# The first of sixteen graphs: adjacency by row block into four free PSUM banks, early weights on ScalarE's queue, inverse roots in two parts

## The chip, the core and the metric

The kernel runs on one core of a Trainium2 chip. A core has TensorE (PE; its weight loads are listed as PEld), VectorE (DVE), ScalarE (ACT), GpSimd (POOL) and SyncE (SP), each with its own instruction stream in program order; they wait for each other by semaphores. Data moves from HBM by DMAs, which are issued from the stream of an engine (SP in the kernel before). The metric is the device time of one execution in microseconds (us); less is better.

## What is computed

Sixteen graphs of 512 nodes and 64 channels pass through four layers, each behind a layer norm and a maximum with 0, each added to x. A batch row is one graph, and the graphs don't depend on each other.

```
h = max(layernorm(x), 0);  x = x + chebyshev(h, adj)   # order 4
h = max(layernorm(x), 0);  x = x + attention(h, adj)   # encoder, 2 attention layers, 3-layer MLP
h = max(layernorm(x), 0);  x = x + gcn(h, adj)
h = max(layernorm(x), 0);  t = adj @ h; x = x + where(t > 0.5, t / t, 0)

chebyshev: d = sum(adj, -1) ** -0.5;  L = I - d[:, None] * adj * d[None, :]
           T0 = I, T1 = L, Tk = 2 L T(k-1) - T(k-2);  out = sum_k Tk @ h @ W[k] + bias
gcn:       rs = sum(adj + I, -1);  di = where(rs > 0, rs ** -0.5, 0)
           out = relu((di[:, None] * (adj + I) * di[None, :]) @ (h @ kernel))
```

## The kernel before, in words

**Tiles.** A graph's adjacency is a_nat, 128 partitions by 4 row blocks by 512 columns (1 MB). TensorE needs it turned: 16 transposes of 128x128 give four column blocks of 128x512, each split into a rounded part at_hi (a copy by ScalarE) and a rest at_lo (a subtraction by VectorE), since products of higher precision are made from both. Slots of three graphs are kept.

**Stages.** A graph passes three rounds. In the first (age 0): norm, turning of adj, row sums and their inverse roots, the products with the Chebyshev weights (cheb_weights), three propagations with folds (cheb_prop3/fold3, prop2/fold2, prop1/fold1), the second norm and the encoder. In the second (age 1): both attention layers. In the third (age 2): MLP, gcn and the last layer. One round handles graph n at age 0, n-1 at age 1 and n-2 at age 2, so in the very first round graph 0 is alone and every engine works on one chain.

**What sets the order.** A table ORDER names, for each engine, the steps of a round in the order in which its stream is written (`turn_a0-0` is turn_a0 of the graph of age 0). `walk` writes them out. Steps of graphs that don't exist in a round are left out.

**Steps named later** (lines of the kernel before). turn_a (L899): four transposes of one column block, from all four row blocks, into bank j % 2 of pre_ps; the third and fourth wait until VectorE has taken the first and second (at_split). copy_at (L521) and row_sum (L535) on ScalarE; row_sum copies a row block and accumulates into rs, and has two records, the ACTIVATE and the read of its accumulator. split_at (L715) on VectorE. Norm: statistics on VectorE (L685 to L691), root and centring on GpSimd (L414, L417), then h_nat and its copy on VectorE (L701, L709). cheb_ht: h is turned (L908), copied (L542) and split (L723). cheb_weights: eight products (L924), then e2, e1, f0 on VectorE (L746 to L749). inverse_roots on GpSimd (L438 to L448): eight small instructions of 128x4, or 128x8 for the power (L441), which makes both d (columns 0 to 3) and di (4 to 7). cheb_u3 on GpSimd (L454 to L462) makes the operand of the first propagation (L936); folds are L953. set_bias_rows (L647 to L658): the value biases of both attention layers, made once, after the first graph's split of its second h_t. Attention: queries L990, keys L995, values L1002 and L1006 with v_n (L580) on ScalarE, scores L1021 to L1025, mask L795 and L803.

**Loads.** SP issues, in this order: x_in and a_nat of graph 0, six early weights (cheb_ws twice, cheb_bs, enc_ws twice, enc_bs; one semaphore early_in), 20 small ones (weights_in), and graphs 1 and 2. Of each weight with 64 rows two copies go to the two partition halves. VectorE's stream begins with a wait for early_in and the splitting of both weights (L668 to L678); only then come the statistics of graph 0.

Of the kernel before, what the change touches and what calls it, by code (L numbers as in the profile page):

```python
# [21 lines left out]
F32 = mybir.dt.float32  # L22
# [36 lines left out]
        norm_cheb-0 add_cheb_bias-0 split_qk.1-1 mask_bias-1 inverse_roots-0 cheb_u3-0  # L59
        norm_gcn-2 split_qk.2-1 cheb_f0-0 norm_last-2 norm_enc-0  # L60
        add_mlp_bias-0""".split(),
# [35 lines left out]
def graph_layers(nc, x, adj, cheb_w, cheb_b, enc_w, enc_b, att_w, att_b, w1, b1, w2, b2, w3, b3,  # L97
# [11 lines left out]
    with ExitStack() as ctx:  # L109
# [112 lines left out]
        weights_split = sem("weights_split")  # L222
        a_loaded = [sem(f"a_loaded{s}") for s in range(SLOTS)]
# [51 lines left out]
        x1b_done = sem("x1b_done")  # L275
        dinv_done = sem("dinv_done")
# [33 lines left out]

        def walk(engine, steps, chains=()):

            order = [(entry[:-2], int(entry[-1])) for entry in ORDER[engine]]
            assert sorted(name for name, _ in order) == sorted(steps), engine

            def one(*graphs):
                for chain in chains:
                    chain.next_round()
                for name, age in order:
# [22 lines left out]
        n_early, n_small = 6, 2 * 6 + 8  # L342
# [4 lines left out]
        def _(sp):  # L347
            early = [(half, cheb_w.rearrange("k o c d -> (o c) k d"))
                     for half in (cheb_ws[0:C], cheb_ws[C:P])]
            early += [(cheb_bs[:], cheb_b.rearrange("a b c -> (a b c)").partition_broadcast(P))]  # L350
            early += [(half, enc_w) for half in (enc_ws[0:C], enc_ws[C:P])]
            early += [(enc_bs[:], enc_b.rearrange("(h o) -> h o", o=1))]
# [10 lines left out]
            assert len(early) == n_early and len(small) == n_small  # L363
# [34 lines left out]
        def _(pool):  # L398
# [32 lines left out]
            def inverse_roots(g):  # L431

                pool.wait_ge(rowsums, 4 * g.n + 4)
                if g.n >= SLOTS:

                    pool.wait_ge(x3_done, g.n - SLOTS + 1)
# [4 lines left out]
                pool_pre.add(gp.tensor_tensor(d[:], rs[:], nhalf[:], ALU.pow))  # L441
# [8 lines left out]
            def cheb_u3(g):  # L450

                pool.wait_ge(dinv_done, g.n + 1)
# [40 lines left out]
            def add_mlp_bias(g):  # L493
# [12 lines left out]
                "inverse_roots": inverse_roots, "cheb_u3": cheb_u3, "cheb_f0": cheb_f0, "norm_enc": scale_norm("pre", 1),  # L506
# [10 lines left out]

# [117 lines left out]
        def _(dve):  # L635
# [38 lines left out]
            for whole, high, low in splits:  # L674
                ve.tensor_copy(high[:], whole).then_inc(weights_split, 1)
# [470 lines left out]
```

## Time and profile before

| | |
|---|---|
| median of three timed runs | 871.86 us (871.08 to 872.88) |
| profiled execution: time, span | 873.75 us, 871.8 us |
| busy: PE, PEld, DVE | 771.5, 543.3, 561.3 us |
| busy: ACT, POOL | 445.4, 357.0 us |
| mean granted TensorE clock | 0.969 of 2.4 GHz |

The span runs from the first to the last instruction record; the execution's own time is 1.95 us longer, and the profiled execution lies 1.89 us above the median. In the steady part one round takes 49.0 us. Rounds 2 to 16 each take in a new graph; two rounds behind them drain.

A row of the timeline reads: start in us, duration, engine and line, operation, output tile <- input tiles, shapes, count, and in brackets the idle time of that engine just before it and what ended it. SPq marks the issue of a DMA. Durations of matmuls include their latency; where they follow each other the starts tell the pace.

### The profile page before, as it was taken

The page shows a single profiled execution, that of the slowest core. Times are in us where ns is not written, and L with a number is a line of the kernel's source. Part 1 is how long each engine was busy: PE and PEld are TensorE (multiplying, and loading weights), DVE is VectorE, ACT ScalarE, POOL GpSimd, SP SyncE. Part 2 cuts the span into 40 slices and gives each one's busy share as a digit, 9 for nine tenths or more (in the row PEclk, how much of TensorE's full clock was granted, in tenths as well). Part 3 has the DMA queues.
Part 4 walks back from the last instruction along what each step waited for, and adds up shares of the span by engine and source line. Part 5 has one row for each costly group of instructions (what it writes and reads, how often), then busy time and mean ns, then how long its engine had stood idle before and what let it go on. Part 6 is the DMA issues. An engine that isn't in the chain of part 4 may idle for free.

```text
span 871.8 us, 11510 instructions
## 1 busy us (share of the span) xinstructions
PE 771.5 (88%) x3808; PEld 543.3 (62%) x3808; DVE 561.3 (64%) x1631; ACT 445.4 (51%) x929; POOL 357.0 (41%) x475
## 2 busy tenths in 40 slices
PE   3649799998999999998999999998999999998864
PEld 2426566675766766675766666675766666675533
DVE  3255667767676767767676767767676767765432
ACT  2035463737474563737474563737474563735430
POOL 3133434536162544536162544536162544532200
PEclk9869899999999999999999999999999999999995
DMA  6100100102010010201020010101020110000000
GB/s 166 45 0 1 43 14 1 61 1 61 1 61 2 21 41 0 61 1 61 1 62 1 18 44 1 61 1 62 1 61 1 18 44 1 7 1 6 1 7 6
DMA packets 29275, 22.77 MB, mean 26 GB/s; under 512 B 19488, under 2 KB 21024, under 8 KB 29216
## 3 DMA queue, kind: packets, MB, share of 16 engines
q1 hardware_dynamic: 29216, 22.03, 8.5%
q8 instruction: 31, 0.51, 0.2%
q14 instruction: 28, 0.23, 0.1%
HBM read 19.93 MB, written 2.10 MB: 25 GB/s over the span
## 4 chain that ended last, share of the span: by engine, by line
PE 52%; issue 16%; POOL 15%; DVE 12%; ACT 4%; POOLq 0%; DVEq 0%
PE turn_ps L1056 13%; PE pre_ps L936 8%; PE post_ps L936 4%; POOL rstd_pre L414 4%; PE pre_ps L953 4%; PE turn_ps L1039 3%; POOL k_lo L486 2%; PE pre_ps L899 2%; DVE h_nat_pre L709 2%; POOL centred_pre L417 2%; DVE score_ps L795 2%; PE qkv_ps L990 2%; DVE h_nat_pre L701 2%; PE qkv_ps L995 2%; PE post_ps L1071 2%
## 5 line engine op out<-in xcount | busy, mean ns | idle before, releaser
L589 ACT ACTIVATE negz<-negz,negmax 128x512 f32<-128x512 f32 x128 | 92.2, 720 | 63.9 <-DVE negmax L803 63.8
L414 POOL TENSOR_TENSOR rstd_post<-vareps_post,nhalf 128x4 f32<-128x4 f32 x32 | 32.8, 1024 | 209.6 <-DVE vareps_post L691 209.6
L1056 PE MATMUL turn_ps<-pt,v_n 128*128 128x512 f32 x256 | 115.2, 592 | 0.0
L795 DVE TENSOR_TENSOR score_ps<-score_ps,a_nat 128x512 f32<-128x512 f32 x128 | 89.1, 696 | 19.4 <-PE score_ps L1025 18.5
L936 PE MATMUL pre_ps<-at_hi,u_pair_pre 128*128 128x512 f32 x192 | 88.4, 461 | 7.2 <-DVE u_pair_pre L731 5.2
L548 ACT ACTIVATE y_t_pre<-pre_ps 128x512 f32<-128x512 f32 x48 | 28.7, 597 | 124.6 <-PE pre_ps L936 124.6
L803 DVE CUSTOM_DVE_ANT_0 negz<-score_ps,gate 128x512 f32<-128x512 f32 x128 | 88.6, 692 | 4.4
L414 POOL TENSOR_TENSOR rstd_pre<-vareps_pre,nhalf 128x4 f32<-128x4 f32 x32 | 33.9, 1060 | 130.7 <-DVE vareps_pre L691 130.7
L596 ACT ACTIVATE pt<-turn_ps 128x512 f32<-128x512 f32 x128 | 74.0, 592 | 17.7 <-PE turn_ps L1039 15.6
L1039 PEld LDWEIGHTS turn_ps<-ident,negz 128*128 128x128 f32 x512 | 61.1, 141 | 32.6 <-issue 16.1
L936 PE MATMUL pre_ps<-at_lo,u_pair_pre 128*128 128x512 f32 x192 | 79.3, 413 | 0.0
L1039 PE MATMUL turn_ps<-ident,negz 128*128 128x128 f32 x512 | 75.9, 276 | 1.9 <-ACT negz L589 1.7
L1056 PEld LDWEIGHTS turn_ps<-pt,v_n 128*128 128x128 f32 x256 | 46.1, 190 | 45.9 <-issue 45.9
L936 PE MATMUL post_ps<-at_hi,u_pair_post 128*128 128x512 f32 x128 | 55.7, 435 | 21.5 <-DVE u_pair_post L731 21.5
L486 POOL TENSOR_TENSOR q_lo<-q_t,q_hi 128x512 fp32r<-128x512 f32 x32 | 43.6, 1363 | 67.1 <-ACT q_t L566 67.1
L1021 PE MATMUL score_ps<-k_hi,q_hi 128*128 128x512 f32 x128 | 63.6, 497 | 6.2 <-DVE negmax L803 6.2
L486 POOL TENSOR_TENSOR k_lo<-k_t,k_hi 128x512 fp32r<-128x512 f32 x32 | 45.9, 1435 | 45.9 <-ACT k_t L566 45.9
L899 PE MATMUL pre_ps<-ident,a_nat 128*128 128x128 f32 x256 | 41.2, 290 | 20.6 <-DVE at_lo L715 13.3
L899 PEld LDWEIGHTS pre_ps<-ident,a_nat 128*128 128x128 f32 x256 | 31.4, 148 | 42.3 <-issue 42.3
L715 DVE TENSOR_TENSOR at_lo<-pre_ps,at_hi 128x512 fp32r<-128x512 f32 x64 | 42.7, 685 | 21.6 <-ACT at_hi L521 21.5
L814 DVE TENSOR_TENSOR h_t<-turn_ps,inv_row 128x512 f32<-128x512 f32 x32 | 22.1, 692 | 50.7 <-PE turn_ps L1056 50.7
L1024 PE MATMUL score_ps<-k_lo,q_hi 128*128 128x512 f32 x128 | 52.6, 411 | 1.6 <-POOL k_lo L486 1.6
(138 smaller groups left out, 1791.5 us busy)
## 6 DMA issues: line engine op xcount, KB each, us to landing
a_nat<-in_adj SPq DMA_DIRECT2D x16, 1024.0 KB, 5.8
x_in<-in_x SPq DMA_DIRECT2D x16, 128.0 KB, 2.6
out<-x_out SPq DMA_DIRECT2D x16, 128.0 KB, 1.9
cheb_ws<-in_L_gnn_weight SPq DMA_DIRECT2D x2, 64.0 KB, 4.9
att_w<-in_L_gnn_a_wv SPq DMA_DIRECT2D x2, 64.0 KB, 2.5
att_w<-in_L_gnn_a_wk SPq DMA_DIRECT2D x2, 64.0 KB, 2.3
att_w<-in_L_gnn_a_wq SPq DMA_DIRECT2D x2, 64.0 KB, 2.2
bv_f<-in_L_gnn_a_bv SPq DMA_DIRECT2D x2, 64.0 KB, 2.7
```

The costliest lines, as they stand in the source:

```text
L414: gp.tensor_tensor(rstd[t][:], vareps[t][:], nhalf[:, 0:RB], ALU.pow)\
L486: gp.tensor_tensor(low[a][:], whole[:], high[a][:].bitcast(F32), ALU.subtract)\
L589: sc.activation(probs[:, i, :], negz[:, i, :], ACT.Exp, bias=negmax[:, i:i + 1], scale=-1.0, accum_out=total[:, i:i + 1]).then_inc(probs_d ...
L596: sc.activation(pt[:, :, i * P:(i + 1) * P], turn_ps[i % 2][:].rearrange("p (j n) -> p j n", n=P), ACT.Copy)\
L795: ve.tensor_tensor(score_ps[i % 2][:], score_ps[i % 2][:], a_nat[s][:, i, :], ALU.mult)\
L803: ve.tensor_tensor_reduce(negz[:, i, :], score_ps[i % 2][:], gate[:, i, :], -1.0, 3.0e38, ALU.add, ALU.min, negmax[:, i:i + 1]).then_inc(b ...
L899: mm = te.transpose(pre_ps[:, j % 2, i * P:(i + 1) * P], a_nat[g.slot][:, i, j * P:(j + 1) * P], ident[:])
L936: mm = te.matmul(bank, u_pair[t][:, j, :, :].rearrange("p a c -> p (a c)"), at[g.slot][:, j, :], start=(j == 0 and at is at_hi), stop=(j = ...
L1021: te.matmul(score_ps[i % 2][:], q_hi[a][:, part], k_hi[a][:], start=True, stop=False)
L1024: te.matmul(score_ps[i % 2][:], q_hi[a][:, part], k_lo[a][:], start=False, stop=False)
L1039: mm = te.transpose(turn_ps[i % 2][:, j * P:(j + 1) * P], probs[:, i, j * P:(j + 1) * P], ident[:])
L1056: mm = te.matmul(turn_ps[0][:], v_n[a][:, j * P:(j + 1) * P], pt[:, j, :], start=(j == 0), stop=(j == RB - 1))
```

## The change

For graph 0 alone there is a second table, FIRST, with the same steps in another order, used in the first round. In it:

- adj comes in four DMAs, one a row block, each with its own semaphore. TensorE turns a row block when it has landed, into four banks (post_ps, qkv_ps, turn_ps0, turn_ps1), which nothing else uses in this round. The first h is turned into score_ps0. So no turn waits for a split, and all at_lo come due at cheb_prop3.
- ScalarE sums three row blocks, copies h_t, sums the fourth, and then makes the four at_hi.
- The six early weights are issued from ScalarE's stream, ahead of its table load, with a semaphore of their own for cheb_ws.
- VectorE begins with the norm; the Chebyshev weights are split behind it, the encoder's behind fold3, and the value biases of layer 1 behind fold3, of layer 2 behind fold2.

For all graphs, inverse_roots is split: `roots` makes d (a power of 128x4), cheb_u3 follows at once, and `more_roots` makes di and the rest behind it (a second power of 128x4). cheb_weights on VectorE waits for root_done, fold3 for dinv_done.

```diff
+FIRST = {
+    "tensor": """
+        turn_a0-0 turn_a1-0 turn_a2-0 cheb_ht-0 turn_a3-0 cheb_weights-0 cheb_prop3-0 cheb_fold3-0
...
-        norm_cheb-0 add_cheb_bias-0 split_qk.1-1 mask_bias-1 inverse_roots-0 cheb_u3-0
+        norm_cheb-0 add_cheb_bias-0 split_qk.1-1 mask_bias-1 roots-0 cheb_u3-0 more_roots-0
...
+        def at_bank(g, j):
+            return (post_ps, qkv_ps, *turn_ps)[j][:] if first(g) else pre_ps[:, j % 2, :]
+        def ht_bank(g, k):
+            return score_ps[0][:] if first(g) and k == 0 else pre_ps[:, 0, :]
...
-            load(Graph(0, 0), False)
+            sp.dma_start(x_in[0][:], x_d[0]).then_inc(x_loaded[0], 16)
+            for i in range(RB):
+                sp.dma_start(a_nat[0][:, i, :], adj_d[0][:, i, :]).then_inc(a_rows_in[i], 16)
...
-            for to, what in early:
-                sp.dma_start(to, what).then_inc(early_in, 16)
...
+            def roots(g):
+                pool.wait_ge(rowsums, 4 * g.n + 4)
+                gp.tensor_tensor(dinv[g.slot][:, 0:RB], rs[:, 0:RB], nhalf[:, 0:RB], ALU.pow)\
+                    .then_inc(root_done, 1)
...
-                pool_pre.add(gp.tensor_tensor(d[:], rs[:], nhalf[:], ALU.pow))
+                pool_pre.add(gp.tensor_tensor(d[:, RB:], rs[:, RB:], nhalf[:, RB:], ALU.pow))
...
+            for half in (cheb_ws[0:C], cheb_ws[C:P]):
+                act.dma_start(half, cheb_w.rearrange("k o c d -> (o c) k d")).then_inc(cheb_in, 16)
+            for to, what in early:
+                act.dma_start(to, what).then_inc(early_in, 16)
...
+            def turn_first_rows(g, i):
+                wait_rows(pe, g, i)
+                for j in range(RB):
+                    mm = te.transpose(at_bank(g, j)[:, i * P:(i + 1) * P],
+                                      a_nat[g.slot][:, i, j * P:(j + 1) * P], ident[:])
+                    if i == RB - 1:
+                        mm.then_inc(at_ready, 1)
...
             def cheb_prop3(g):
+                if first(g):
+                    pe.wait_ge(at_split, RB)
```

Three places in the streams show it. First VectorE's stream in graph 0, before: from the split of the weights to e2 (at_lo0 is the rest of graph 0's turned adj, h_t the turned h).

```order
L678 TENSOR_TENSOR cheb_lo<-cheb_ws,cheb_hi 128x192 [waits weights_split]
L678 TENSOR_TENSOR enc_lo<-enc_ws,enc_hi 128x128
L685 BN_STATS stats_pre<-x_in0 128x6 [waits x_loaded0]
L685 BN_STATS stats_pre<-x_in0 128x6 x3
L688 BN_AGGR meanvar_pre<-stats_pre 128x2 [waits dve_pre]
L688 BN_AGGR meanvar_pre<-stats_pre 128x2 x3
L691 TENSOR_SCALAR vareps_pre<-meanvar_pre 128x4 [waits dve_pre]
L701 SCALAR_TENSOR_TENSOR h_nat_pre<-centred_pre,rstd_pre 128x4x64 [waits rstd_done_pre]
L709 COPY h_nat_pre<-h_nat_pre 128x4x64 [waits dve_pre]
L715 TENSOR_TENSOR at_lo0<-pre_ps,at_hi0 128x512 [waits at_copied] x4
L723 TENSOR_TENSOR h_t<-pre_ps,h_t 64x512 [waits ht_copied]
L746 TENSOR_TENSOR e2<-pre_ps,dinv0 128x256 [waits dinv_done,cheb_ready]
```

The same stretch of VectorE's stream now; the norm stands ahead of these rows.

```order
L720 SCALAR_TENSOR_TENSOR cheb_ws<-cheb_ws 128x64 [waits cheb_in]
L722 TENSOR_TENSOR cheb_ws<-cheb_ws 128x64
L712 CAST cheb_hi<-cheb_ws 128x192 [waits weights_split]
L714 TENSOR_TENSOR cheb_lo<-cheb_ws,cheb_hi 128x192 [waits weights_split]
L772 TENSOR_TENSOR h_t<-score_ps0,h_t 64x512 [waits ht_copied]
L764 TENSOR_TENSOR at_lo0<-post_ps,at_hi0 128x512 [waits at_copied]
L764 TENSOR_TENSOR at_lo0<-qkv_ps,at_hi0 128x512 [waits at_copied]
L795 TENSOR_TENSOR e2<-pre_ps,dinv0 128x256 [waits root_done,cheb_ready]
L796 TENSOR_TENSOR e1<-pre_ps,dinv0 128x256
L798 TENSOR_TENSOR f0<-pre_ps,x_b 128x256 [waits xb_done]
L764 TENSOR_TENSOR at_lo0<-turn_ps0,at_hi0 128x512 [waits at_copied]
L764 TENSOR_TENSOR at_lo0<-turn_ps1,at_hi0 128x512 [waits at_copied]
```

The weights moved from ahead of the norm to behind it, h_t moved ahead of all at_lo, and two at_lo stand behind f0.

Second, ScalarE's stream in graph 0, before: the last at_hi and row sum (junk, rs), then h_t and the copies of the propagations.

```order
L521 ACTIVATE at_hi0<-pre_ps 128x512 [waits at_ready]
L535 ACTIVATE junk,rs<-a_nat0 128x512 [waits rowsums]
L542 ACTIVATE h_t<-pre_ps 128x512 [waits ht_ready]
L548 ACTIVATE y_t_pre<-pre_ps 128x512 [waits y_ready_pre] x3
L542 ACTIVATE h_t<-pre_ps 128x512 [waits ht_ready]
```

ScalarE's stream from its last early DMA to the first propagations' copies now:

```order
L563 DMA enc_bs<-in_L1_gnn_enc_b 128x1
L583 ACT_TABLE_LOAD
L583 ACTIVATE junk,rs<-a_nat0 128x512 [waits a_rows_in0]
L583 ACTIVATE junk,rs<-a_nat0 128x512 [waits rowsums,a_rows_in1]
L583 ACTIVATE junk,rs<-a_nat0 128x512 [waits rowsums,a_rows_in2]
L590 ACTIVATE h_t<-score_ps0 128x512 [waits ht_ready]
L583 ACTIVATE junk,rs<-a_nat0 128x512 [waits rowsums,a_rows_in3]
L568 ACTIVATE at_hi0<-post_ps 128x512 [waits at_ready]
L568 ACTIVATE at_hi0<-qkv_ps 128x512 [waits at_ready]
L568 ACTIVATE at_hi0<-turn_ps0 128x512 [waits at_ready]
L568 ACTIVATE at_hi0<-turn_ps1 128x512 [waits at_ready]
L596 ACTIVATE y_t_pre<-pre_ps 128x512 [waits y_ready_pre] x3
```

All four at_hi now stand behind h_t and the four row sums.

Third, GpSimd's stream in graph 0 before, from x_b (x plus bias) to the operand u_pair_pre; the rows from L438 on come again for every graph.

```order
L428 TENSOR_TENSOR x_b<-x_in0,cheb_bs 128x256 [waits early_in,x_loaded0]
L438 TENSOR_SCALAR rs<-rs 128x4 [waits rowsums]
L439 TENSOR_SCALAR positive<-rs 128x4
L441 TENSOR_TENSOR dinv0<-rs,nhalf 128x8 [waits pool_pre]
L443 TENSOR_TENSOR dinv0<-dinv0,positive 128x4 [waits pool_pre]
L444 TENSOR_SCALAR d_neg<-dinv0 128x4
L445 TENSOR_TENSOR d_root<-dinv0,rs 128x4
L446 TENSOR_SCALAR d_m2<-dinv0 128x4
L448 TENSOR_TENSOR d_m2<-d_m2,dinv0 128x4 [waits pool_pre]
L454 TENSOR_TENSOR u3<-h_nat_pre,dinv0 128x256 [waits h_ready_pre,dinv_done]
L460 CAST u_pair_pre<-u3 128x4x64 [waits pool_pre]
L462 TENSOR_TENSOR u_pair_pre<-u3,u_pair_pre 128x4x64 [waits pool_pre]
```

GpSimd's stream there now (one more row, the last d_m2, follows):

```order
L460 TENSOR_TENSOR x_b<-x_in0,cheb_bs 128x256 [waits early_in,x_loaded0]
L466 TENSOR_TENSOR dinv0<-rs,nhalf 128x4 [waits rowsums]
L491 TENSOR_TENSOR u3<-h_nat_pre,dinv0 128x256 [waits h_ready_pre,root_done]
L497 CAST u_pair_pre<-u3 128x4x64 [waits pool_pre]
L499 TENSOR_TENSOR u_pair_pre<-u3,u_pair_pre 128x4x64 [waits pool_pre]
L475 TENSOR_SCALAR rs<-rs 128x4
L476 TENSOR_SCALAR positive<-rs 128x4
L478 TENSOR_TENSOR dinv0<-rs,nhalf 128x4 [waits pool_pre]
L480 TENSOR_TENSOR dinv0<-dinv0,positive 128x4 [waits pool_pre]
L481 TENSOR_SCALAR d_neg<-dinv0 128x4
L482 TENSOR_TENSOR d_root<-dinv0,rs 128x4
L483 TENSOR_SCALAR d_m2<-dinv0 128x4
```

The three instructions of u3 moved from behind all the roots to behind the first power.

## Rows read from the trace of the kernel before

**Rows 1.** The page's head: span of the profiled execution.
```profile
span 871.8 us, 11510 instructions
```
**Rows 2.** Chain that ended last: start us, us, what.
```profile
23.86 3.77 PE pre_ps L936 x8
...
124.68 1.86 PE pre_ps L936 x8
```
**Rows 3.** Stretch 40 to 60 us: busy of engines, PEclk granted, DMA share, GB/s.
```profile
40.00:60.00 20.00, 11.18 (x30) 6.83 (x30) 9.40 (x42) 3.63 (x6) 3.06 (x5) 0.52 0.00 0
```
**Rows 4.** Timeline of all engines, 0 to 23 us.
```profile
0.72 1.28 ACT L521 ACT_TABLE_LOAD   x1 [0.72 <-PEq L1130]
0.72 0.45 SPq L370 DMA_DIRECT2D x_in<-in_x  x1
...
7.27 1.94 PE L899 MATMUL pre_ps<-ident,a_nat 128*128 128x128 f32 x8 [7.27 <-DMA a_nat<-in_adj]
...
8.55 0.23 DVE L668 SCALAR_TENSOR_TENSOR cheb_ws<-cheb_ws 128x64 f32<-128x64 f32 x1 [5.33 <-DMA enc_bs<-in_L_gnn_enc_b]
...
9.86 0.60 DVE L685 BATCH_NORM_STATS2 stats_pre<-x_in 128x6 f32<-128x64 f32 x4
...
11.15 1.03 POOL L414 TENSOR_TENSOR rstd_pre<-vareps_pre,nhalf 128x4 f32<-128x4 f32 x1 [8.19 <-DVE vareps_pre L691]
...
13.77 0.29 DVE L709 COPY h_nat_pre<-h_nat_pre 128x256 f32<-128x256 f32 x1
...
14.81 1.94 PE L899 MATMUL pre_ps<-ident,a_nat 128*128 128x128 f32 x8 [5.60 <-DVE at_lo L715]
...
17.31 1.11 PE L908 MATMUL pre_ps<-ident,h_nat_pre 128*128 128x128 f32 x4 [0.56 <-DVE at_lo L715]
17.52 0.63 ACT L535 ACTIVATE junk<-a_nat 128x512 bf16<-128x512 f32 x1
...
18.46 0.60 ACT L542 ACTIVATE h_t<-pre_ps 128x512 fp32r<-128x512 f32 x1 [0.23 <-PE pre_ps L908]
...
18.98 1.66 POOL L441 TENSOR_TENSOR dinv<-rs,nhalf 128x8 f32<-128x8 f32 x1
...
19.84 0.53 PE L924 MATMUL pre_ps<-cheb_hi,h_t 128*128 128x192 f32 x1 [1.42 <-DVE h_t L723]
...
21.91 0.42 DVE L746 TENSOR_TENSOR e<-pre_ps,dinv 128x256 f32<-128x256 f32 x1 [2.12 <-PE pre_ps L924]
```
**Rows 5.** DMA view, issues from 0 to 1 us: KB each, us from issue to landing.
```profile
x_in<-in_x SPq DMA_DIRECT2D x1, 128.0 KB, 2.3
```
**Rows 6.** Waits, 0 to 60 us: in total, times, longest us.
```profile
DVE tmp L777 <- PE pre_ps L953: 6.5, 1, 6.5
...
DVE tmp L766 <- PE pre_ps L953: 5.2, 1, 5.2
```
**Rows 7.** Timeline of the second round, 53 to 68 us.
```profile
53.78 0.71 DVE L647 CAST bv_rows<-bv_f 1x128 bf16<-1x128 f32 x3
...
59.43 0.59 DVE L685 BATCH_NORM_STATS2 stats_pre<-x_in 128x6 f32<-128x64 f32 x4
...
63.33 1.24 DVE L709 COPY h_nat_pre<-h_nat_pre 128x256 f32<-128x256 f32 x1
...
63.44 0.60 ACT L580 ACTIVATE v_n<-qkv_ps 128x512 f32<-128x512 f32 x1
...
65.44 1.66 PE L899 MATMUL pre_ps<-ident,a_nat 128*128 128x128 f32 x8 [2.18 <-DVE at_lo L715]
...
67.83 0.69 DVE L715 TENSOR_TENSOR at_lo<-pre_ps,at_hi 128x512 fp32r<-128x512 f32 x1 [0.40 <-ACT at_hi L521]
```
**Rows 8.** Timeline of a steady round, 314 to 321 us.
```profile
314.97 0.69 DVE L803 CUSTOM_DVE_ANT_0 negz<-score_ps,gate 128x512 f32<-128x512 f32 x1
...
315.70 0.73 POOL L462 TENSOR_TENSOR u_pair_pre<-u,u_pair_pre 128x256 fp32r<-128x256 f32 x1
...
320.56 0.48 PE L936 MATMUL pre_ps<-at_hi,u_pair_pre 128*128 128x512 f32 x1
```

More of the change, by code:

```diff
@@ L318, in one @@
                     chain.next_round()
-                for name, age in order:
+                for name, age in fill if graphs[1:] == (None, None) else order:
                     g = graphs[age]
@@ L347, in _ @@
         def _(sp):
[L348 to L352, printed above, removed]
             small = []
@@ L362, in _ @@
             small += [(half, gcn_w) for half in (gcn_ws[0:C], gcn_ws[C:P])]
-            assert len(early) == n_early and len(small) == n_small
+            assert len(small) == n_small
             def load(g, waits=True):
@@ L516, in _ @@
             sc = nc.scalar
+            early = [(cheb_bs[:], cheb_b.rearrange("a b c -> (a b c)").partition_broadcast(P))]
+            early += [(half, enc_w) for half in (enc_ws[0:C], enc_ws[C:P])]
+            early += [(enc_bs[:], enc_b.rearrange("(h o) -> h o", o=1))]
+            assert len(early) == n_early
+            for half in (cheb_ws[0:C], cheb_ws[C:P]):
+                act.dma_start(half, cheb_w.rearrange("k o c d -> (o c) k d")).then_inc(cheb_in, 16)
+            for to, what in early:
+                act.dma_start(to, what).then_inc(early_in, 16)
             def copy_at(j):
@@ L526, in f @@
                 def f(g):
+                    if i == 0 or first(g):
+                        wait_rows(act, g, i)
                     if i == 0:
-                        act.wait_ge(a_loaded[g.slot], 16 * (g.round + 1))
                         if follows(g):
@@ new lines, in set_bias_rows, with split_weights @@
+                for i in range(1, RB):
+                    ve.tensor_copy(bv_rows[a][0:96, i, :], bv_rows[a][0:96, 0, :])\
+                        .then_inc(bias_rows, 1)
+                    made += 1
+                assert made == (a + 1) * n_bias_rows // 2
+            def split_weights(whole, high, low, made):
+                ve.tensor_copy(high[:], whole).then_inc(weights_split, 1)
+                dve.wait_ge(weights_split, made + 1)
+                ve.tensor_tensor(low[:], whole, high[:].bitcast(F32), ALU.subtract)\
+                    .then_inc(weights_split, 1)
@@ L673, in _ @@
-            splits = ((cheb_ws[:, 0:K - 1, :], cheb_hi, cheb_lo), (enc_ws[:], enc_hi, enc_lo))
-            for whole, high, low in splits:
-                ve.tensor_copy(high[:], whole).then_inc(weights_split, 1)
-            dve.wait_ge(weights_split, 5)
-            for whole, high, low in splits:
-                ve.tensor_tensor(low[:], whole, high[:].bitcast(F32), ALU.subtract)\
-                    .then_inc(weights_split, 1)
             def norm_stats(t, chain, g, k, src):
@@ L722, in split_ht @@
                 dve.wait_ge(ht_copied, 2 * g.n + k + 1)
-                ve.tensor_tensor(h_t[C:P, :], pre_ps[C:P, 0, :], h_t[C:P, :].bitcast(F32),
+                ve.tensor_tensor(h_t[C:P, :], ht_bank(g, k)[C:P, :], h_t[C:P, :].bitcast(F32),
                                  ALU.subtract).then_inc(ht_split, 1)
-                if first(g) and k == 1:
-                    set_bias_rows()
             def split_u(t, chain, u):
@@ L739, in cheb_norm @@
                 norm_apply("pre", dve_pre, g, 0)
+                if first(g):
+                    combine_cheb_weights()
             def cheb_weights(g):
@@ L770, in cheb_fold2 @@
                 split_u("pre", dve_pre, c1)
+                if first(g):
+                    set_bias_rows(1)
             def cheb_fold1(g):
```

123 lines of the change are left out of this document (77 added, 46 removed).

## Prediction

> **What bounds the kernel now.** I read the page's head first, then the chain that ended last, since only time on that chain can be won. The span is 871.8 us [rows 1]; the table ahead gives PE as busy for 771.5 of it, and the chain runs through TensorE in the steady rounds. The change hardly touches these rounds, so the second view is the timeline of the start, where graph 0 is alone. There nothing is full: one chain hops over the engines until the first propagation (L936) starts at 23.86 [rows 2]. The rows to see, in order [rows 4]: x_in is issued at 0.72 and lands 2.3 later [rows 5], so at 3.0, but VectorE stands still 5.33 us until 8.55 for enc_bs, the last of the early weights, and takes up x_in only at 9.86. Adj has landed at 7.27, TensorE turns two column blocks, and then waits 5.60 us, until 14.81, for at_lo, which stands behind the norm in VectorE's stream (the norm's last piece starts at 13.77). Behind that come h_t, the Chebyshev products and e2 at 21.91. The third view is the second round [rows 7]: VectorE makes the bias rows from 53.78, so the norm of graph 1 begins at 59.43, its last copy ends at 64.57, and TensorE waits 2.18 us until 65.44 for the at_lo behind it.
>
> From 40 to 60 us the granted clock is 0.52, that is nearly all at the 1.2 GHz level [rows 3]. The first propagation takes 3.77, a later one 1.86 [rows 2]: by that pace it ran at the same level. I keep the start at it throughout.
>
> **Term 1: the start of the first propagation.** All durations are those of [rows 4] unless another group is named.
>
> VectorE: statistics can start at 3.3, when x_in is there and the cast of ident is done. From their start to the end of the norm's copy before: 9.86 to 14.06, so 4.2. The h is ready at 7.5. Four of the six weight instructions follow; all six took 9.86 - 8.55 = 1.3, so I give them 1.0, to 8.5. They are needed only for the products, two microseconds later.
>
> Transfers: adj landed at 7.27, the early weights at 8.55. The 1.28 between them is what the early weights cost behind adj. Now they compete with it. If none of them gets ahead of the last row block it lands at 7.2, if all do at 8.5; I take 7.9, and 7.0 for the third. In these rows the transfers of one queue only are seen, so the share is my choice of the middle.
>
> For that place the Trainium skill, page "DMA: Bandwidth & Descriptors", section "Issuing engines are not separate DMA queues", says that DMAs from different engines run on the same 16 DMA engines and interleave, and that issuing from several saves only the time of issuing. The trace before has one queue and can't show it; the rule speaks against the move of the early weights, and by it the last block would stand at the late end, 8.5, and the sum below would lose nothing to 0.5.
>
> TensorE: a row block takes 0.97 (half of 1.94). The third is turned at 8.0. h is turned from 8.0, with ScalarE's copy 1.15 after the start of the turn (18.46 - 17.31): copy from 9.15 to 9.75. The fourth block is turned meanwhile, to about 10.
>
> ScalarE: six issues of DMAs stand ahead of its table load. Nearest row is SP's issue of x_in, 0.45; up to 0.7 each as bound. So 0.7 + 2.7 to 4.2, and 1.28 for the table: free at 4.7 to 6.2. A row sum is 0.63 and its accumulator 0.2, three are 2.5: done at 8.7 at the latest, before the copy of h_t at 9.15. The fourth ends at 10.5. Four at_hi of 0.6, which overlap by 0.1, end at 12.6.
>
> VectorE: split of h_t 9.75 to 10.45 (0.69 as at_lo [rows 7]). TensorE's eight products took 19.84 to 21.91, so 2.1: to 12.55. In this time two at_lo are made. Then e2, e1, f0, three of 0.42 with overlap and wait, 1.1: to 13.65. Then two at_lo, 1.3: to 14.95. The first propagation starts at 15.0.
>
> GpSimd: power of 128x4 from 10.5, 1.03 by the row of rstd (L414); the three of u3 before ended at about 23.8 and began after d_m2, 2.0: ready at 13.6. VectorE is later, so GpSimd hides behind it with 1.4 to spare.
>
> 23.86 - 15.0 = 8.9. Bounds: 7.5, if every choice above is at its late end, and 9.7, if transfers cost nothing and VectorE finds all at_hi waiting.
>
> **Term 2: bias rows out of the second round.** They take 59.43 - 53.78 = 5.65. Their halves, 2.8 each, and the encoder's split (0.5) go into VectorE's waits of 5.2 (before L766) and 6.5 (before L777) [rows 6]. 3.3 in 5.2 and 2.8 in 6.5 fit: nothing, as long as the clock is low. In the second round the norm is then done at 53.8 + 4.2 = 58.0 instead of 64.57. What is late next is ScalarE: its stream has v_n from 63.44 to 64.04 ahead of the third at_hi, and TensorE has its values ahead of the third turn. Before, the third turn began at 65.44 and its copy some 0.65 later, at 66.1; now the copy can begin at 63.95. So the last at_lo (67.83) comes 2.1 earlier, and with it the first mask. I take 2.0 of the 5.65; bounds 1.0 and 2.7. These times are all on the old clock of the start; they come 8.9 earlier.
>
> **Term 3: roots in two parts, 16 graphs.** One power of 1.66 becomes two of 1.03, +0.4 on GpSimd a graph. In a steady round the operand is ready at 316.43 and TensorE takes it at 320.56 [rows 8]: 4.1 us to spare, before and after. So 0. Bounds: 0 to +0.4 a graph, 6 in all, if GpSimd's stream set the round; I take the cover of 4.1 and go by 0. DMAs of graphs 1 and 2 start some 2.7 earlier, as six issues have left SP's queue, and are needed 30 us later: 0.
>
> The moved three instructions of u3 now lie beside other work of VectorE. The row that warns is the copy at 63.33, which takes 1.24 beside GpSimd's work instead of 0.29 [rows 4, 7]. Where they lay before, L803 kept its 0.69 beside them [rows 8], and 2.2 us earlier come a multiplication by inv_row and the same L795 and L803, all with an operand in PSUM: 0. In graph 0, x_b can fall onto the weight split: at most 0.7, and between its end at 8.5 and the products at 10.45 there is 1.9 to spare.
>
> The Trainium skill, "SBUF — State Buffer", section "SBUF: two separate sides", has the rule: GpSimd and a VectorE instruction with two SBUF inputs or in a two-port mode lock each other out of a shared port for the whole instruction. By that rule, too, the three instructions cost nothing beside VectorE's reads of PSUM; the 1.24 of the copy agrees with it.
>
> **Sum.** 8.9 + 2.0 + 0 = 10.9. Against the profiled execution: span 871.8 - 10.9 = 860.9, and with the 1.95 around it 862.85. That execution is 1.89 above the median of the runs, so the median is forecast at 871.86 - 10.9 = 861.0 us.
>
> **Rivals.**
> (A) The transfers hold the start. With pieces of adj and early weights mixed, the third row block lands at 9 instead of 7. Then h_t is turned at 10 and all behind it is 2 later. For it: adj needed 7.27 even alone at the head of its queue. Against it: the third block needs only three quarters of adj to be through. Gain 8 to 9: 863.4.
> (B) The clock. The start before ran at the low level. A denser TensorE could get the high level earlier. A propagation is then 3.77 - 1.86 = 1.9 shorter; two of them on the chain give 3.8, less some 0.5 since the bias rows no longer fit into VectorE's wait. 857.7. For it: the turns, h_t and products are packed into 8 us. Against it: the chain of three propagations, with its gaps, is the same, and the level was low with it from 40 to 60.
> (C) Slower: the three instructions of u3, moved by 2.2 us in each steady round, lock out VectorE on the path from attention's multiplication to the mask. Price by the copy's rows: 1.24 - 0.29 = 0.95 a graph, in 15 graphs 14.3, less the 10.9: 875.3. It decides from 0.73 a graph. Against it speaks L803's 0.69 beside the same three instructions.
> (D) The change doesn't do what it says: the first propagation starts as before, since another wait ends last (early weights from ScalarE land as late as 8.5 and the Chebyshev split with them, with the table load and row sums behind). But even with all of them at 8.5 the start is 16.5, so little is left for it: 871.
>
> **How the numbers follow.** Forecast 0.62, A 0.17, B 0.13, C 0.04, D 0.04. The forecast's own spread comes from 7.5 to 9.7 and 1.0 to 2.7, so 859.5 to 863.4. For 8 in 10 I go on half way into B at the low side and over A at the high side: 858.5 to 864.3. What a measurement of this kernel can tell from no change is about 0.2%, 1.7 us. Faster: forecast, A, B, 0.92; the same: D, 0.04; slower: C, 0.04.
>
> **What would show it.** In the profile after: statistics of graph 0 at about 3.3; h turned at about 8; the first propagation at 15.0, released by VectorE's last at_lo and not by GpSimd or a DMA; no bias rows behind the second h_t; the norm of graph 1 finished before its first at_hi; last at_lo of graph 1 some 11 us earlier than 67.83; steady rounds of 49.0 us as before. It is wrong if a row block's DMA releases the h_t turn late (A), if a propagation before 40 us takes under 3 us (B), if the round is longer than 49.1 (C), or if the first propagation starts after 17 (D).

## The result, and the profile after

The changed kernel takes 860.58 us (median of 4 runs, 858.40 to 862.05) against 872.02 for the kernel before on the same chip: a ratio of 0.987 (95% interval 0.984 to 0.989), 11.4 us faster. The forecast was 861.0, from 10.9. The profiled execution after has a span of 859.1. One execution of the kernel with the roots in one part (below), 1093.49 us at a granted clock of 0.652, is a slow run and is left out of that kernel's median.

The start is read first. The timeline of the kernel after, graph 0, all engines (start, duration, engine, line; in brackets the idle time before and what ended it):

```profile
3.32 0.61 DVE L734 BATCH_NORM_STATS2 stats_pre<-x_in 128x6 f32<-128x64 f32 x4
4.65 1.28 ACT L583 ACT_TABLE_LOAD   x1 [4.65 <-issue]
5.09 0.45 PE L950 MATMUL post_ps<-ident,a_nat 128*128 128x128 f32 x1 [5.09 <-DMA a_nat<-in_adj]
...
6.74 0.29 DVE L758 COPY h_nat_pre<-h_nat_pre 128x256 f32<-128x256 f32 x1
...
8.03 0.47 PE L950 MATMUL post_ps<-ident,a_nat 128*128 128x128 f32 x1 [1.00 <-DMA a_nat<-in_adj]
...
8.94 1.06 PE L976 MATMUL score_ps<-ident,h_nat_pre 128*128 128x128 f32 x4
...
10.04 0.60 ACT L590 ACTIVATE h_t<-score_ps 128x512 fp32r<-128x512 f32 x1 [1.30 <-PE score_ps L976]
10.67 0.69 DVE L772 TENSOR_TENSOR h_t<-score_ps,h_t 64x512 fp32r<-64x512 f32 x1 [2.68 <-ACT h_t L590]
11.32 1.02 POOL L466 TENSOR_TENSOR dinv<-rs,nhalf 128x4 f32<-128x4 f32 x1 [1.42 <-ACT junk L583]
11.42 0.53 PE L994 MATMUL pre_ps<-cheb_hi,h_t 128*128 128x192 f32 x1 [0.56 <-DVE h_t L772]
...
13.48 0.42 DVE L795 TENSOR_TENSOR e<-pre_ps,dinv 128x256 f32<-128x256 f32 x1 [0.42 <-PE pre_ps L994]
13.59 0.73 POOL L499 TENSOR_TENSOR u_pair_pre<-u,u_pair_pre 128x256 fp32r<-128x256 f32 x1
...
14.48 1.28 DVE L764 TENSOR_TENSOR at_lo<-turn_ps,at_hi 128x512 fp32r<-128x512 f32 x2
15.81 0.79 PE L1006 MATMUL pre_ps<-at_hi,u_pair_pre 128*128 128x512 f32 x1 [2.38 <-DVE at_lo L764]
```

Against [rows 4]: VectorE takes up x_in at 3.32 instead of 9.86, and h is ready at 7.03. TensorE turns two row blocks from 5.09 and stands still 1.00 for the third, so the gap of 5.60 for at_lo is gone. The first propagation starts at 15.81 instead of 23.86, released by VectorE's last at_lo, with GpSimd's operand ready 1.5 earlier (14.32).

TensorE behind it, in the same execution: the first fold and the queries, the first products of graph 0's attention.

```profile
20.28 1.97 PE L1023 MATMUL pre_ps<-cheb_ws,y_t_pre 128*128 128x64 f32 x8 [0.69 <-ACT y_t_pre L596]
...
48.10 2.04 PE L1064 MATMUL qkv_ps<-h_t,att_w 128*128 128x512 f32 x2 [0.93 <-ACT h_t L606]
```

The queries of the kernel before:

```profile
55.96 2.04 PE L990 MATMUL qkv_ps<-h_t,att_w 128*128 128x512 f32 x2 [0.93 <-ACT h_t L558]
```

VectorE in the second round of the kernel after:

```profile
24.67 0.70 DVE L694 CAST bv_rows<-bv_f 1x128 bf16<-1x128 f32 x3
...
31.62 1.68 DVE L694 CAST bv_rows<-bv_f 1x128 bf16<-1x128 f32 x3
...
45.92 0.60 DVE L734 BATCH_NORM_STATS2 stats_pre<-x_in 128x6 f32<-128x64 f32 x4
...
49.83 0.29 DVE L758 COPY h_nat_pre<-h_nat_pre 128x256 f32<-128x256 f32 x1
52.02 0.69 DVE L764 TENSOR_TENSOR at_lo<-pre_ps,at_hi 128x512 fp32r<-128x512 f32 x1 [1.90 <-ACT at_hi L568]
...
57.80 0.69 DVE L764 TENSOR_TENSOR at_lo<-pre_ps,at_hi 128x512 fp32r<-128x512 f32 x1 [0.41 <-ACT at_hi L568]
58.41 0.69 DVE L851 TENSOR_TENSOR score_ps<-score_ps,a_nat 128x512 f32<-128x512 f32 x1
```

The bias rows now lie at 24.67 and 31.62, in VectorE's waits. The last at_lo stands at 57.80; in [rows 7] it stands at 67.83. Of the 10.03 between them 7.86 were won before (queries at 48.10, before 55.96), so the second round gives 2.17 in this pair. The first mask (L851) starts at 58.41. The copy at 49.83 takes 0.29; in [rows 7] it took 1.24, beside GpSimd's work.

The rest: from graph 0's x_out (its output) to graph 13's are 637.00 us, or 49.00 a round (before 637.43, or 49.03). The profiled pair is 12.7 apart (871.8 and 859.1), more than the medians. Of that, 10.0 lie ahead of the first mask, 1.5 between it and graph 0's x_out (84.25 and 85.75), 0.4 in the 13 rounds, and 0.8 behind them, where the last fold took 1.10 after and 1.97 before. The 1.5 isn't put down to the change: the same stretch takes 83.92 in one kernel with the old order below and 85.0 in two with the new one.

### The profile page after: what moved, and what is told of

The parts are those of the page before. It is cut to its first block, busy times and chain, and to the rows that moved or that the text cites. A ratio compares the mean times of both kernels' runs of the same rounds, so it can differ in the third digit from the quotient of the medians.

```text
span 859.1 us, 11501 instructions
## 1 busy us (share of the span) xinstructions
PE 764.4 (89%) x3776; PEld 540.5 (63%) x3808; DVE 560.9 (65%) x1631; ACT 445.9 (52%) x929; POOL 364.0 (42%) x491
## 4 chain that ended last, share of the span: by engine, by line
PE 53%; issue 15%; POOL 14%; DVE 12%; ACT 5%; DMA 1%; POOLq 0%; SPq 0%; ACTq 0%; DVEq 0%
PE turn_ps L1130 13%; PE pre_ps L1006 8%; PE post_ps L1006 4%; PE pre_ps L1023 4%; POOL rstd_pre L446 3%; PE turn_ps L1113 3%; POOL k_lo L523 2%; PE qkv_ps L1064 2%; PE pre_ps L967 2%; DVE h_nat_pre L758 2%; POOL centred_pre L449 2%; DVE score_ps L851 2%; PE qkv_ps L1069 2%; PE post_ps L1145 2%; PE pre_ps L994 2%
## 5 line engine op out<-in xcount | busy, mean ns | idle before, releaser
L851 DVE TENSOR_TENSOR score_ps<-score_ps,a_nat 128x512 f32<-128x512 f32 x128 | 89.1, 696 | 18.9 <-PE score_ps L1099 18.0
L764 DVE TENSOR_TENSOR at_lo<-pre_ps,at_hi 128x512 fp32r<-128x512 f32 x60 | 40.1, 685 | 22.9 <-ACT at_hi L568 22.9
L1006 PE MATMUL post_ps<-at_lo,u_pair_post 128*128 128x512 f32 x128 | 52.3, 408 | 0.0
L1099 PE MATMUL score_ps<-k_hi,q_lo 128*128 128x512 f32 x128 | 50.7, 396 | 0.0
```

What stands on the lines that cost most here:

```text
L851: ve.tensor_tensor(score_ps[i % 2][:], score_ps[i % 2][:], a_nat[s][:, i, :], ALU.mult)\
L1006: mm = te.matmul(bank, u_pair[t][:, j, :, :].rearrange("p a c -> p (a c)"), at[g.slot][:, j, :], start=(j == 0 and at is at_hi), stop=(j = ...
L1099: te.matmul(score_ps[i % 2][:], q_lo[a][:, part], k_hi[a][:], start=False, stop=True)\
```

## The experiments

Each starts from the changed kernel unless said otherwise. Times are medians.

**One part put back: early weights behind the row blocks, all from SyncE**

```
-                act.dma_start(half, cheb_w...)   # and four more, on ScalarE
+                sp.dma_start(half, cheb_w...)    # behind the four a_rows
```

> The changed kernel, but the six early weights are issued by SyncE right behind the four row blocks of the adjacency instead of by ScalarE beside them. Theory (the early weights share the transfers and held the third row block until 8.03 us): the third block is turned at 7.0 or before, ScalarE's table load starts at about 0.7 instead of 4.65, and the first propagation starts at 14.8 instead of 15.81, so the time is some 0.9 us under the changed kernel, 859.7. Rival 1 (the adjacency is as late without them): third block still at 8.0, start 15.8, same time. Rival 2 (the weights now land too late for VectorE's split, which the Chebyshev products need by 11.4): products after 11.8, start later than 15.8, time 861 to 862.

Measured: 859.12 us. Its timeline, TensorE:

```profile
6.76 0.48 PE L949 MATMUL post_ps<-ident,a_nat 128*128 128x128 f32 x1
...
8.27 0.27 PE L949 MATMUL post_ps<-ident,a_nat 128*128 128x128 f32 x1
...
13.72 0.50 PE L1005 MATMUL pre_ps<-at_hi,u_pair_pre 128*128 128x512 f32 x1 [2.74 <-DVE at_lo L763]
...
15.13 0.63 PE L1005 MATMUL pre_ps<-at_lo,u_pair_pre 128*128 128x512 f32 x1
```

The third row block is turned at 6.76 instead of 8.03: issued beside the adjacency, the early weights had cost it 1.3 us in this pair. The landing itself varies: in the six kernels here with the weights on ScalarE's queue an engine takes up the third block at 7.57 to 8.12, in the three with the weights behind the rows at 6.74, 6.14 and 6.04. The two groups don't overlap, so the cost is shown, and its size is 0.8 to 2.1. The propagation starts 2.09 earlier, of which 1.27 is the block; the rest comes with a pace nobody had forecast: a turn of 128 columns takes 0.27 from 8.27 on instead of 0.42, and the first four matmuls of the propagation are fast, the others slow. (The next kernel has its products at this pace too, and its propagation starts at 14.83, so against it 1.1 are left.) By time the two kernels can't be told apart (1.5 us; ratios to before 0.985 and 0.987, with intervals that overlap), so the theory is shown by the landing and not by the median. Rival 2 is excluded: VectorE did wait for the Chebyshev weights until 7.89, and the products still began at 9.85.

**One part put back: bias rows behind the second h_t**

```
-                    set_bias_rows(0)        # in cheb_fold3; (1) in cheb_fold2
+                if first(g) and k == 1:     # in split_ht, as before
+                    set_bias_rows(0)
+                    set_bias_rows(1)
```

> The changed kernel, but both halves of the bias rows are made behind the second split of h_t of graph 0 again, where they stood before. Theory: the first propagation stays at 15.8, queries at 48.1 or a little earlier; the norm of graph 1 then waits for them and the first mask comes at 60.6 instead of 58.4: 2.2 us slower than the changed kernel, 862.8. Rival 1 (they cost nothing in the second round, the clock's later start made the difference): first mask 58.4, same time. Rival 2 (the piece that ran slowly beside GpSimd in VectorE's waits held the encoder's norm): queries over 0.5 earlier than 48.1 and a cost of 1.7 or less.

Measured: 861.85 us, 1.3 over the changed kernel. Its VectorE:

```profile
43.77 0.71 DVE L694 CAST bv_rows<-bv_f 1x128 bf16<-1x128 f32 x3
...
49.42 0.59 DVE L734 BATCH_NORM_STATS2 stats_pre<-x_in 128x6 f32<-128x64 f32 x4
...
53.32 1.24 DVE L758 COPY h_nat_pre<-h_nat_pre 128x256 f32<-128x256 f32 x1
...
58.83 0.69 DVE L851 TENSOR_TENSOR score_ps<-score_ps,a_nat 128x512 f32<-128x512 f32 x1
```

The norm of graph 1 starts behind them and the 1.24 of the copy is back. From queries to first mask are 12.88 instead of 10.31, 2.6 more. But this execution reached its queries 2.15 earlier (45.95). The kernel with two waits in the other order (below) has the rows where the changed kernel has them, its queries as early (45.72), and 11.73 to the mask; against it the late rows cost 1.15. The mechanism is shown; its size is 1.1 to 2.6, with 1.3 in the median. The time falls under rival 2, but its reason doesn't hold, since the earlier queries aren't VectorE freed of the rows: 0.98 of the 2.15 lie ahead of the first propagation (14.83), 0.30 are its last matmuls and 0.87 one more fold at the fast pace (1.10 instead of 1.97 for eight products).

**Banks without the row blocks: turned by column, once all has landed**

```
-    wait_rows(pe, g, i); for j: ...at_bank(g, j)[:, i*P:...]
+    if i == 0: wait for all four; for i: ...at_bank(g, j)[:, i*P:...]
```

> The changed kernel, but graph 0's adjacency is turned by column block into the four free banks once all four row blocks are there, instead of by row block as they land. Transfers, banks and VectorE's order are as in the changed kernel. Theory: the last block lands at about 8.8, three columns take 2.6, so h_t is turned at 11.4 instead of 8.94, and all behind it comes 2.5 later: first propagation 18.3, time 863.1. Rival (VectorE's order and ScalarE's copies set the start, the turns have slack): first propagation within 0.5 of 15.8, time within 0.5 of the changed kernel.

Measured: 863.71 us, TensorE released so:

```profile
8.57 1.09 PE L952 MATMUL post_ps<-ident,a_nat 128*128 128x128 f32 x4 [8.57 <-DMA a_nat<-in_adj]
...
18.03 0.80 PE L1007 MATMUL pre_ps<-at_hi,u_pair_pre 128*128 128x512 f32 x1 [2.37 <-DVE at_lo L764]
```

2.2 later at the propagation and 3.1 in the median: turning as the blocks land is worth 2 to 3 us here. (The intervals of the two ratios, 0.987 to 0.993 and 0.984 to 0.989, overlap at their ends, so the propagation is the better evidence.) The turns have no slack.

**The order of VectorE alone, in the kernel before**

```
-            dve.wait_ge(early_in, 16 * n_early)   # and the six weight instructions, ahead of all graphs
+                if first(g): weights_ready()       # the same, behind graph 0's norm
```

> The kernel before, with one edit: VectorE combines and splits the early weights behind the norm of graph 0 instead of ahead of its statistics. Two banks, whole adjacency in one transfer, weights by SyncE. Theory (order on VectorE gives about half of the 8.05 us): statistics at 3.3, weights split from 8.55 to 9.9, first at_lo to 10.6, third turn at 10.6 instead of 14.81, first propagation 4.2 earlier, 19.7, time 867.8. Rival 1 (the wait for at_lo was only nominal, the banks and the transfer set the start): less than 2 us. Rival 2 (order is nearly all of it): first propagation before 17.5, 6 us or more.

Measured: 868.65 us, 3.5 under the kernel before. Its VectorE and TensorE:

```profile
3.15 0.60 DVE L686 BATCH_NORM_STATS2 stats_pre<-x_in 128x6 f32<-128x64 f32 x4
...
8.83 0.23 DVE L669 SCALAR_TENSOR_TENSOR cheb_ws<-cheb_ws 128x64 f32<-128x64 f32 x1 [1.97 <-DMA enc_bs<-in_L_gnn_enc_b]
...
11.53 1.94 PE L902 MATMUL pre_ps<-ident,a_nat 128*128 128x128 f32 x8 [1.71 <-DVE at_lo L716]
...
20.59 0.77 PE L939 MATMUL pre_ps<-at_hi,u_pair_pre 128*128 128x512 f32 x1 [2.01 <-POOL u_pair_pre L462]
```

The wait for at_lo shrinks from 5.60 to 1.71, the propagation comes 3.27 earlier. It fell 0.9 short of the expectation: the adjacency landed at 7.88, the weights at 8.83, and one weight instruction took 0.78 instead of about 0.2. So of the 8.05 of the start, VectorE's order alone makes 3.3 and turning row by row 2.2; the remaining 2.6 belong to the free banks, the earlier root and the transfers. These two runs don't tell them apart; the next one prices the root at 1.0 to 2.0, and the early weights' queue takes something off again. What the free banks alone are worth isn't shown. Nor need the parts add up: one edit was put into the kernel before, the others taken out of the changed one.

**Roots in one part again**

```
-    dinv[:, 0:RB] = pow(rs) ; then_inc(root_done)      # roots
-    ... d[:, RB:] = pow(rs[:, RB:])                     # more_roots
+    ... d[:] = pow(rs[:]) ...                           # one chain, waits on dinv_done
```

> The changed kernel with the inverse roots of all 16 graphs taken in one part again (one power of 8 columns, and u3, e2 and e1 wait for the whole chain of GpSimd's small operations). Theory: in graph 0 the operand of the first propagation is ready 2.0 later than 14.32, at 16.3, so the first propagation starts 0.5 later; the steady round goes from 49.00 back to 49.03, which is 0.45 us in 13 rounds; together 1.0 us slower than the changed kernel. Rival 1 (the split has nothing to do with the shorter round): round stays 49.00, 0.5 us slower. Rival 2 (the second power costs on GpSimd): round 48.97 or less, not slower.

Measured: 860.92 us (859.75 to 861.81, 4 runs), 0.3 over the changed kernel. Its VectorE and TensorE:

```profile
14.47 0.43 DVE L789 TENSOR_TENSOR e<-pre_ps,dinv 128x256 f32<-128x256 f32 x1 [1.81 <-POOL d_m L479]
...
16.81 0.79 PE L999 MATMUL pre_ps<-at_hi,u_pair_pre 128*128 128x512 f32 x1 [4.65 <-DVE at_lo L758]
```

The operand is ready at 16.32, as expected, but it isn't what ends last: e has to wait for the whole chain, until 14.47, and the two at_lo behind it end at 16.76. The propagation starts 1.0 later than in the changed kernel. Against the kernel with late bias rows, which had its third row block as early (7.57, here 7.64) and its products at the same pace, it is 2.0 later (14.83). So the split is worth 1.0 to 2.0 at the start, not 0.5. The steady round is 48.98, not 49.03: the shorter round isn't the roots'. In the medians, 0.3 apart with an interval of about 2 us, nothing of this can be seen, and the expected 1.0 is neither confirmed nor excluded.

**Two waits in the other order**

```
-                    if j >= 2: pe.wait_ge(at_split, ...)
                     wait_rows(pe, g, 0)
+                    if j >= 2: pe.wait_ge(at_split, ...)
```

> The changed kernel with one edit that touches no computation: from graph 1 on, TensorE's third and fourth turn of the adjacency wait for the adjacency first and for at_lo second, as in the kernel before (in the changed kernel it is the other way round). Theory (this order makes the 0.05 us by which the steady round is shorter, since TensorE waits there for at_lo): round 49.03 to 49.04 instead of 48.98 to 49.00, and 0.6 us slower. Rival (the round is shorter for another reason): round 49.00 or less.

Measured: 860.93 us, round 49.03. TensorE's third turn in a steady round, of this kernel and then of the changed one:

```profile
295.13 1.23 PE L967 MATMUL pre_ps<-ident,a_nat 128*128 128x128 f32 x8 [0.41 <-DVE at_lo L764]
```

```profile
295.80 1.26 PE L967 MATMUL pre_ps<-ident,a_nat 128*128 128x128 f32 x8 [0.32 <-DVE at_lo L764]
```

The wait is 0.09 longer when at_lo stands second in the code, and the round 0.034 longer (637.44 over 13 rounds against 637.00). The other profiles agree: the median of this wait over the steady rounds is 0.40 or 0.41, and the round 49.03 to 49.04, in the four kernels that wait for the adjacency first; it is 0.31 or 0.32, and the round 48.98 to 49.00, in the eight that wait for at_lo first. So this side effect of rewriting turn_a makes the 0.4 us; the medians, 0.35 apart, can't resolve it.

**TensorE's waits filled**

```
+            def fill(g, n):          # graph 0 only: 4 to 60 ahead of a wait, 202 in all
+                for _ in range(n):
+                    te.matmul(score_ps[1][:, 0:P], ones_bf[:], ones_bf[:], ...)
```

> The changed kernel with TensorE's waits in graph 0's first passage filled by products of ones_bf with itself (128 columns, some 190 in all) into a bank that nobody reads then; results are unchanged. Theory (TensorE runs at the 1.2 GHz pace in the first 50 us because it stands still between short stretches of work, as rival B had it): the three propagations take 1.9 instead of 3.8, folds and the encoder's products halve too, queries start 8 to 9 us before 48.1, and the time is 7 to 10 us under the changed kernel, 852. Rival 1 (the level does not follow from the work in these waits): paces as in the changed kernel, and the fillers that overrun a wait make it 1 to 4 us slower. Rival 2 (the gain is given back later by a longer stretch at 1.2 GHz): queries much earlier, but the distance between first mask and the end longer, gain under 3.

Measured: 852.89 us, 7.7 under the changed kernel. Its TensorE:

```profile
14.52 0.50 PE L1013 MATMUL pre_ps<-at_hi,u_pair_pre 128*128 128x512 f32 x1 [1.73 <-DVE at_lo L764]
14.85 0.39 PE L1013 MATMUL pre_ps<-at_lo,u_pair_pre 128*128 128x512 f32 x1
15.09 0.40 PE L1013 MATMUL pre_ps<-at_hi,u_pair_pre 128*128 128x512 f32 x1
...
20.21 0.50 PE L1013 MATMUL pre_ps<-at_hi,u_pair_pre 128*128 128x512 f32 x1 [0.65 <-DVE u_pair_pre L778]
```

The windows of TensorE (busy time of each engine, then the granted clock), of the changed kernel and then of the filled one:

```profile
5.00:30.00 25.00, 17.41 (x60) 13.48 (x60) 11.04 (x34) 7.45 (x16) 7.22 (x15) 1.00 0.52 152
...
32.00:50.00 18.00, 9.74 (x25) 6.04 (x26) 9.31 (x37) 1.88 (x3) 5.49 (x8) 0.50 0.00 0
```

```profile
32.00:50.00 18.00, 12.28 (x109) 9.08 (x106) 8.77 (x27) 9.18 (x20) 10.26 (x11) 1.00 0.00 0
```

The propagations run at the 2.4 GHz pace (matmuls of 512 columns 0.23 to 0.24 apart instead of 0.43, and 2.1 for a propagation instead of 3.8) and the queries come at 39.29 instead of 48.10. The theory holds: 8.8 at the queries, 9.8 at the first mask, 7.7 in the median, where no run of this kernel (851.08 to 853.36) is as long as the shortest of the changed one (858.40). Where the 2 us between mask and median went isn't shown. So the low pace of this start followed from TensorE standing still in its waits; the next run shows that filling them doesn't always prevent it.

**Both: early weights behind the row blocks, and fillers**

The two edits above together.

> The same fillers on the kernel whose early weights are issued by SyncE behind the row blocks. There the products of graph 0 and half of its first propagation already ran at the 2.4 GHz pace (0.24 us for 512 columns, 0.43 behind 15.1). Theory: the level stays high from about 8 us on, queries 8 us before that kernel's 44.0, and 7 to 9 us under its 859.1: 851. Rival 1: no change of pace, 859 to 862. Rival 2 (given back later): queries early, gain under 3.

Measured: 850.10 us (849.65 to 854.10, 5 runs), 9.0 under the one without fillers and the best median of all: ratio to the kernel before 0.976 (0.974 to 0.978). The level isn't sure: in the profiled execution, the slowest of the five (854.10), the first propagation ran at the slow pace (matmuls 0.43 apart from 14.01 on), and the queries, at 40.33, are later than with fillers alone. The kernel of the next experiment has the same first round, and its profile has the fast pace throughout, with queries at 38.56:

```profile
13.77 0.50 PE L1012 MATMUL pre_ps<-at_hi,u_pair_pre 128*128 128x512 f32 x1 [1.72 <-DVE at_lo L763]
...
38.56 1.10 PE L1082 MATMUL qkv_ps<-h_t,att_w 128*128 128x512 f32 x2 [0.47 <-ACT h_t L605]
```

**Fillers in the last graph too**

This one starts from the kernel just above, with 148 more fillers in the last graph.

```
+                fill(g, 8, B - 1)    # ahead of each MLP product; 56 ahead of a propagation, 6 ahead of a fold
```

> The kernel with early weights behind the row blocks and fillers in graph 0, and in addition fillers in TensorE's waits of the last graph, from its MLP to its last fold (148 products of 128 columns in the same bank, free by then). Theory (the pace of 0.43 us for 512 columns behind 827 us comes from those waits, as at the start): the last two propagations take 1.9 instead of 3.8, the last part, from graph 14's output to graph 15's, goes from 34.6 to 31, and the time is 3 us under 850.1: 847. Rival 1 (fillers overrun the waits and give that back): 849 to 851. Rival 2 (the level at the end has another cause, such as the high load of the 700 us before): pace unchanged, no gain.

Measured: 850.97 us (849.38 to 851.11). Its last propagation and fold:

```profile
838.78 0.50 PE L1012 MATMUL post_ps<-at_hi,u_pair_post 128*128 128x512 f32 x1 [2.03 <-DVE u_pair_post L777]
...
840.78 0.63 PE L1012 MATMUL post_ps<-at_lo,u_pair_post 128*128 128x512 f32 x1
...
842.10 1.97 PE L1029 MATMUL post_ps<-fold,y_t_post 128*128 128x64 f32 x8
```

From graph 14's x_out to graph 15's are 32.73 instead of 34.57 (34.3 to 35.4 in all the kernels without these fillers), so 1.8 of the 3 expected, until the level falls at 840.3 in spite of the fillers. In the median nothing is seen: 0.9 over the 850.10, inside the band of rival 1, whose cause no row shows. Inconclusive as to time.

**The kernel before, filled**

The same edit on the kernel before, with 34 fillers ahead of the first turn, 42 ahead of the third and 15 ahead of the first propagation, 249 in all.

> The kernel before with fillers in TensorE's waits of graph 0 (some 215, more in the two long waits there), results unchanged. It holds the clock equal on both sides of the comparison with the changed kernel with fillers (852.89). Theory (the change's gain is its start and its second round, and the clock adds or takes little on average): before with fillers 863 to 864, 10 to 11 over the filled changed kernel, first propagation at 22 to 23 with a pace of 0.24. Rival 1 (a good part of the 11.4 us was a better clock with the change): below 861. Rival 2 (fillers gain less in before, so the change and the fillers work together): above 866.

Measured: 866.59 us (863.67 to 867.14, 6 runs), 5.6 under the kernel before. Its TensorE:

```profile
14.62 1.68 PE L905 MATMUL pre_ps<-ident,a_nat 128*128 128x128 f32 x8 [3.61 <-DVE at_lo L715]
...
24.27 0.63 PE L943 MATMUL pre_ps<-at_hi,u_pair_pre 128*128 128x512 f32 x1
...
25.44 0.40 PE L943 MATMUL pre_ps<-at_lo,u_pair_pre 128*128 128x512 f32 x1
```

Rival 2 came true, narrowly (its bound was 866). The long wait was left with 3.61 us unfilled (the 42 fillers ran through it fast, in 2.51), the granted clock was 0.50 from 15 to 25, and the first propagation starts at 23.28, half of it at the slow pace. Filled, the two kernels are 13.7 apart, unfilled 11.4. So a better clock with the change doesn't explain its gain (rival 1): 8.8 of the 13.7 lie at the first propagation, 1.3 between it and the queries, where only this kernel has slow matmuls, and from queries to first mask are 9.36 us in the filled changed kernel and 12.45 here, 3.1 where the change's second term gave 2.2 at the slow pace. Fillers sized for this kernel's waits weren't tried.

## Why the prediction was right, step by step

**The bound.** Right: the chain over the engines in the start was where the time could be won.

**Term 1 was mis-sized, 8.05 instead of 8.9.** The failing step is the share of the early weights in the transfers, which I had said was "my choice of the middle": the third block came at 8.03 and not at 7.0. Behind it the forecast distances held: h_t turned at 8.94 (8.0), its copy at 10.04 (9.15), products done at 13.44 (12.55), last at_lo done at 15.76 (14.95). The offset stays at 0.8 to 0.9 all the way. So the truth lay between the forecast and rival A, which had the block at 9. The weights on ScalarE's queue are a part of the change that costs time: with them behind the rows in one queue the block was turned 1.27 earlier.

The rule of the Trainium skill, "DMA: Bandwidth & Descriptors", section "Issuing engines are not separate DMA queues", that DMAs from different engines interleave on the same 16 DMA engines, was the better guide: by it I had put the last block at 8.5, and in the kernel turned by column, with the same transfers, TensorE had all four at 8.57.

One distance was too long and hidden: the norm took 3.7 and not 4.2, since h_nat's first instruction took 0.43 instead of 0.93, so h was ready at 7.03 and waited for the third block. ScalarE was free at 5.93, inside 4.7 to 6.2, and hidden as forecast. GpSimd was ready at 14.32 instead of 13.6, 1.5 before VectorE; with the roots in one part the start is 1.0 to 2.0 later, by e and not by the operand.

**Term 2: 2.17 instead of 2.0**, by the landmarks of the two profiles. The halves fitted into the waits; 2.05 and 2.30 of wait were left behind them. Three casts together took 1.68 beside a subtraction and a product by GpSimd (0.70 otherwise) and were hidden too. What was late next was ScalarE's at_hi, as said. But the 2.17 hold for one pace only. In the kernel before and in the two made from it (VectorE's order alone, and filled), queries to first mask take 12.45 to 12.49, whatever TensorE's pace. With the new order it is TensorE's pace that sets it: 11.73 and 11.76 where queries and keys both ran slow, 10.3 to 10.6 where the queries did and the keys mostly not, 9.4 with both fast. So the term is worth 0.7 to 3.1, and that the two profiles to be compared had the same pace there was luck.

**Term 3: 0 for the roots was right** for the steady rounds. Rival C is excluded, since the round didn't grow (49.00). Not foreseen were the 0.4 us of the two waits in turn_a.

**Rival B** had the wrong cause for this kernel and the right lever. In its profile the denser start didn't lift the pace (0.43 from 16.4 to 27; one fold of three fast, as before). In near copies it did in part: the one with two waits swapped had all three folds fast, and the one with the early weights behind the rows had a first propagation of 2.89, under B's sign of 3. The whole level could be had, for 7.7 us, by filling waits.

**The sum**: 8.05 + 2.17 + 0.43 = 10.65, against 11.4 measured by medians with an interval of about 2 us either way. That the total came within 0.5 of the forecast is in part luck: term 1 was 0.85 too large, and 0.17 of term 2 and the 0.43 of the two waits, which nobody had in the sum, made up for most of it.

## What to carry to other kernels

When a start-up chain hops over engines, take the distances behind the first landing from the rows, and spend the care on the landing: they held to 0.2 us while the landing was off by 1.0. Small transfers that are needed later belong behind the large one that is needed first, not on another engine's queue: here that brought the landing 0.8 us or more forward, which the medians could not resolve. And where TensorE waits in short gaps at a program's start, look at the spacing of equal matmuls: here idle waits at the start cost 7.7 us, nearly as much as the whole change had won there. Before a difference between two profiles is put down to an edit, compare the pace of equal matmuls in both.

## What the runs showed of the hardware

In the first 30 us of the changed kernel the granted clock reads 1.00, while matmuls of 512 columns come 0.43 apart, the pace of the stretch where it reads 0.50; in the filled kernel, also at 1.00, they come 0.24 apart from 14.5 on. At the start of these programs the spacing tells the level and the granted clock doesn't.

The start isn't the same from one execution to the next, though nothing in it was edited. The kernel with late bias rows differs from the changed one only behind its first propagation, but had turned h_t 0.46 us earlier by then (8.48 and 8.94). The kernel with two waits in the other order has the very same first round, and its first fold ran at the fast pace, its queries 2.38 earlier than the 48.10:

```profile
20.14 1.10 PE L1023 MATMUL pre_ps<-cheb_ws,y_t_pre 128*128 128x64 f32 x8 [0.69 <-ACT y_t_pre L596]
...
45.72 2.05 PE L1064 MATMUL qkv_ps<-h_t,att_w 128*128 128x512 f32 x2 [0.93 <-ACT h_t L606]
```

So a difference under some 2.4 us between two single profiles of the start isn't put down to an edit here, unless a row names its cause.

The order of two waits in front of one TensorE instruction costs 0.09 us a time where the wait that ends last stands second (0.40 to 0.41 against 0.31 to 0.32, in all twelve profiles).
